# Three layers of one Trainium2 kernel: from three blocks to one block with handed-over beginnings

## The reference, cut to what matters

```python
x = x + L0(x)   # attention, 16 heads; dense or sparse per batch, by u_prev
x = x + L1(x)   # gates and causal running sums ("traces"), then a layer norm
x = x + L2(x)   # gelu(x W1 + b1) times W2, and a part of W2 chosen per batch ("expert")
x = x + L3(x)   # softmax((x + embed[stage]) keys^T) keys

# L1, cut:
ctx = causal_ema(x, tau_ctx)
gated = x * sigmoid([x, ctx] Wg^T + bg)
mod = 0.5 + sigmoid(gelu(x Wn1^T + bn1) Wn2^T + bn2)             # 32 columns
temporal = sum_d softmax(blend)_d * causal_ema(gated * mod_d, tau_d)   # 32 decays
out = (gelu(x Wsoma^T) * sigmoid(temporal Wtemp^T)) Wout^T
return layernorm(out) * gamma + beta
```

## Time and profile before

| | before |
|---|---|
| median of 3 runs | 1950.69 us (1947.42 to 1953.83) |
| the profiled execution | 1952.55 us, span 1950.9 us |
| attention layer (to its last value product) | 0 to 741.5 us |
| first layer edge (to `lags(0, 0, 0)`) | 741.5 to 785.2 us |
| trace layer's loop (to the last `turn_back`) | 785.2 to 1404.5 us |
| second layer edge (to `output(0, ., 0)`) | 1404.5 to 1453.3 us |
| last part | 1453.3 to 1950.9 us |
| busy: PE, DVE, ACT, POOL | 93%, 76%, 61%, 36% |

### The profile page before, as it was taken

One profiled execution on the slowest core, in us unless ns is written; L12 is line 12 of the kernel. 1 busy time (PEld: TensorE's weight loads), 2 busy tenths in 40 slices (PEclk: granted clock), 3 DMA queues, 4 the chain that ended last, 5 costly groups with the idle time before them and its releaser, 6 DMA issues. The chain is left out here.

```text
span 1950.9 us, 44118 instructions
## 1 busy us (share of the span) xinstructions
PE 1814.3 (93%) x14926; PEld 1462.5 (75%) x14926; DVE 1486.1 (76%) x2206; ACT 1194.9 (61%) x2493; POOL 711.0 (36%) x690
## 2 busy tenths in 40 slices
PE   4899999999999995999999999999749999999997
PEld 4566666666666653788888888888649999999997
DVE  6888998899889996878787878787526666666664
ACT  2677777777777764466666666666535555555553
POOL 5255555555555544333333333334101111111111
PEclk9999999999999996999999999999969999999998
DMA  3233333333333331000000000000031222222221
GB/s 101 92 121 125 110 119 119 124 114 115 122 121 116 114 95 46 1 1 0 0 0 0 0 0 0 0 0 0 1 97 58 80 88 74 73 73 78 86 78 47
DMA packets 104946, 126.25 MB, mean 65 GB/s; under 512 B 27840, under 2 KB 70464, under 8 KB 104896
## 3 DMA queue, kind: packets, MB, share of 16 engines
q1 hardware_dynamic: 86912, 102.72, 16.3%
q0 software_dynamic: 17408, 22.61, 3.7%
q10 hardware_dynamic: 576, 0.26, 0.1%
HBM read 56.54 MB, written 9.44 MB: 34 GB/s over the span
## 5 line engine op out<-in xcount | busy, mean ns | idle before, releaser
L445 DVE TENSOR_REDUCE a_top<-a_s 128x4 f32<-128x1024 f32 x256 | 309.7, 1211 | 75.6 <-PE a_s L708 68.6
L561 ACT ACTIVATE a_e<-a_t 128x512 f32<-128x512 f32 x512 | 276.1, 590 | 134.5 <-PE a_t L722 133.9
L455 DVE SCALAR_TENSOR_TENSOR a_e<-a_e,a_w_t 128x1024 f32<-128x1024 f32 x256 | 316.1, 1236 | 4.7 <-ACT a_e L561 4.7
L1818 ACT ACTIVATE c_hid<-c_pH,c_b 128x256 f32<-128x256 f32 x256 | 107.4, 471 | 189.5 <-PE c_pH L1881 189.1
L1058 POOL TENSOR_TENSOR b_decayed<-b_scratch,b_mod_t 128x1024 f32<-128x1024 f32 x64 | 124.1, 1962 | 206.5 <-ACT b_mod_t L1276 206.5
L737 PE MATMUL a_v<-a_e,a_v_pad 128*32 128x256 f32 x2048 | 165.4, 396 | 23.7 <-DVE a_e L455 20.9
L1442 PE MATMUL b_pS<-b_gated_t,b_decayed 128*128 128x256 f32 x768 | 183.3, 389 | 1.5 <-issue 0.2
L1881 PE MATMUL c_pH<-c_x_hi,c_w_hi 128*128 128x256 f32 x512 | 151.0, 295 | 22.3 <-DVE c_w_lo L1783 22.1
L703 PE MATMUL a_s<-a_absent,a_eye 64*128 64x512 bf16 x1024 | 156.8, 385 | 7.3 <-DMA a_absent<-b_bl_rep 5.4
L1696 POOL TENSOR_TENSOR c_w2b_lo<-c_we,c_w2b_hi 128x512 fp32r<-128x512 f32 x32 | 54.6, 1707 | 290.0 <-ACT c_w2b_hi L1811 290.0
L1442 PEld LDWEIGHTS b_pS<-b_gated_t,b_decayed 128*128 128x128 f32 x768 | 142.0, 192 | 24.1 <-issue 7.0
(11 more groups left out here) (273 smaller groups left out, 5447.1 us busy)
## 6 DMA issues: line engine op xcount, KB each, us to landing
a_st<-a_split SPq DMA_DIRECT2D x384, 128.0 KB, 2.1
b_wsoma<-in_xT SPq DMA_DIRECT2D x32, 256.0 KB, 3.7
x_all<-in_xT SPq DMA_DIRECT2D x32, 256.0 KB, 3.7
a_r_rep<-a_r_rows POOLq DMA_DIRECT2D x64, 128.0 KB, 3.7
c_we<-in_we SPq DMA_DIRECT2D x32, 256.0 KB, 2.8
c_key_t<-in_keyT SPq DMA_DIRECT2D x32, 256.0 KB, 3.2
c_value<-in_key SPq DMA_DIRECT2D x32, 256.0 KB, 2.7
out<-c_y POOLq DMA_DIRECT2D x32, 256.0 KB, 3.2
```

What stands on the lines that cost most here:

```text
L445: dve.tensor_reduce(top[:, qc, half].rearrange("p (r j c) -> p r j c", r=2, j=2)[:, :, cc], ps_s[g % 2][:], AX.X, ALU.max)\
L455: dve.scalar_tensor_tensor(out=buf[:], in0=buf[:], scalar=BIG, in1=w_t[par][:, kc].unsqueeze(1).to_broadcast([P, 4, S]), op0=ALU.min, op1= ...
L561: act.activation(e[g % E_BUFS][:, 2 * r:2 * r + 2], ps_t[r][:], ACT.Exp).then_inc(exp_done, 1)
L1818: ins = act.activation(hid[r % 2][:, i], pH[r][:, i], ACT.Gelu, bias=b1[:, 2 * r + i:2 * r + i + 1])
```

## The change

The three layers stand in one `Block`. Each layer's function now returns its engines' programs instead of running them; those of the second and third layer are generators. An engine's attention program gets the trace program as `then`, and calls `next(then)` at fixed places of its tail; each call emits the trace program's instructions up to its next `yield`. The trace program does the same with the last part's program. What remains is emitted at the end (`finish`). So a layer's tail and the next layer's head stand mixed in one instruction stream per engine.

The comments at the right of the added lines are put in here and say what the call emits; a call of `next(then)` in a last part's stretch works alike.

```diff
     # attention, GpSimd, after the batches
-        for half in range(2):
-            denominators(NB - 1, 1, half)
+        denominators(NB - 1, 1, 0)
+        next(then)                  # memset h1, low_x(0), low wn1, low wg
+        denominators(NB - 1, 1, 1)
         residual(NB - 3)
         compact(NB - 1)
         merge(NB - 1, 1)
+        next(then)                  # low_context(0)
         reciprocal_rows(NB - 1)
+        next(then)                  # decays(0, 0), low_x(1, 1)
         spread(NB - 1)
+        next(then)                  # low_context(1), low wsoma, low wtemp
         residual(NB - 2)
         residual(NB - 1)
-        pool.wait_ge(x1_done, NB)
...
     # attention, VectorE, after the batches
         weigh(NB - 1, 1, GROUPS - 1)
-        ahead_steps = trace_vector(dve, ahead)
-        next(ahead_steps)
+        next(then)                  # context(0), w_rep, w_lag
         normalize(NB - 2, 0)
-        next(ahead_steps)
         reciprocal(NB - 1)
-        next(ahead_steps)
+        next(then)                  # modulation(0), gating(0), low_steps, context(1), body(0) to lag_sum 2
         normalize(NB - 1, 1)
-        next(ahead_steps)
...
     # attention, TensorE, after the batches
+        next(then)                  # turn bl_rep
         mix_values(NB - 1, 1, GROUPS - 2)
         mix_values(NB - 1, 1, GROUPS - 1)
+        next(then)                  # hidden(0, 0)
         for n in (NB - 2, NB - 1):
             for m in range(C):
                 project_out(n, n % 2, m)
+            if n == NB - 2:
+                next(then)          # gate_in(0) ... turn(0), body(0) to modulate_rows(1)
...
     # trace, VectorE
+            if is_batch(n, NB - 1):
+                next(then)          # in body(31), after lag_sum 3: low w1, low_x(0)
...
-        loop(dve, body)
+        yield from loop(dve, body)
+        next(then)                  # split(0, 0)
         low_temporal(NB - 1)
+        next(then)                  # low parts of w2a and of the first w2b
         mixing(NB - 1)
+        next(then)                  # split(0, 1), low part of the second w2b
         low_mixed(NB - 1)
+        next(then)                  # split(0, 2), low_x(1), split(0, 3)
         norm(NB - 1)
...
     # trace, TensorE
+            if is_batch(n, NB - 1):
+                next(then)          # in body(31), after states 3: hidden(0, ., 0)
...
+        next(then)                  # hidden(0, ., 1), hidden(0, ., 2)
         gate_out(NB - 1)
+        next(then)                  # hidden(0, ., 3), hidden(1, ., 0), output(0, ., 0)
         output(NB - 1)
+        next(then)                  # hidden(1, ., 1), output(0, ., 1), hidden(1, ., 2), output(0, ., 2)
         turn_normed(NB - 1)
...
     # build_program
+        with nc.Block() as block:
+            @block.vector
+            def _(dve):
+                last = final.vector(dve)
+                second = trace.vector(dve, last)
+                attention.vector(dve, second)
+                finish(second)
+                finish(last)
```

More of the change, by code:

```diff
@@ L609, in body @@
                     projected(n - 2)
+                if g == 4 and not maxi:
+                    next(ahead_steps)
+                if g in (3, 6) and not maxi:
+                    next(then)
         act.wait_ge(set_up, LAM)
@@ L879, in trace_vector @@
     taus = [(tile["tau_c"], ahead.sp_c), (tile["tau_col"], ahead.sp_col), (tile["tau_row"], ahead.sp_row)]
-    blend_t, wout, table = tile["blend_t"], tile["wout"], ahead.table
+    blend_t, table = tile["blend_t"], ahead.table
     def link(ins):
@@ L892, in trace_vector @@
         link(dve.tensor_scalar(tau[:], tau[:], 80.0, None, ALU.min))
-    link(dve.tensor_reduce(ahead.bl_max[:], blend_t[:], AX.X, ALU.max, negate=True))
     yield
@@ L898, in trace_vector @@
     yield
+    dve.wait_ge(ahead.d_tab, 16 * len(TRACE_TABLES) + 16)
+    link(dve.tensor_reduce(ahead.bl_max[:], blend_t[:], AX.X, ALU.max, negate=True))
     dve.wait_ge(ahead.a_set, 2)
@@ L1087, in _, with vector @@
         low_weight(1, wg, wg_p)
+        yield
         low_context(0)
+        yield
+        decays(0, 0)
+        before.mixed_all(pool)
+        low_x(1, 1)
+        yield
+        low_context(1)
         low_weight(2, wsoma, wsoma_p)
         low_weight(3, wtemp, wtemp_p)
-        decays(0, 0)
-        low_context(1)
-        loop(pool, body)
+        yield
+        yield from loop(pool, body)
+        next(then)
         residual(NB - 1)
-        pool.wait_ge(x2_done, NB)
-    @block.vector
-    def _(dve):
+    def vector(dve, then):
         done = [0]
@@ L1543, in _ @@
         turn(0, 0)
-        pe.wait_ge(w_lo, 4)
-        pe.wait_ge(set_done, 1)
-        loop(pe, body)
+        before.banks_free(pe, "columns")
+        pe.wait_ge(early_done, 2)
+        yield from loop(pe, body)
+        next(then)
         gate_out(NB - 1)
+        next(then)
         output(NB - 1)
+        next(then)
         turn_normed(NB - 1)
+    return handover, Programs(None, gpsimd, vector, scalar, tensor)
 HIDDEN = 1024
@@ L1680, in body, with gpsimd @@
             if ahead:
-                load(n + 1, 1 - par)
-        load(0, 0)
-        loop(sp, body)
-    @block.gpsimd
-    def _(pool):
+                if not is_batch(n, 0):
+                    load_expert(n + 1, 1 - par)
+                load_keys(n + 1, 1 - par)
+            yield from ()
+        before.gates_all(sp)
+        sp.dma_start(w2[:], t["w2"].rearrange("(k p) e -> p k e", p=P)).then_inc(d_w2, 16)
+        load_expert(0, 0)
+        load_expert(1, 1)
+        before.states_all(sp)
+        sp.dma_start(embed_all[:], t["embed"].partition_broadcast(P)).then_inc(d_emb_all, 16)
+        before.added(sp, NB)
+        sp.wait_ge(d_emb_all, 16)
+        load_keys(0, 0)
+        yield from loop(sp, body)
+    def gpsimd(pool):
         def store(n, par):
@@ L1943, in body @@
                 mix_values(n - 1, 1 - par)
-        for r in range(ROUNDS):
-            hidden(0, 0, r)
-        pe.wait_ge(w_lo, 2)
-        loop(pe, body)
+        before.banks_free(pe, "pA")
+        pe.wait_ge(w_lo, 1)
+        hidden(0, 0, 0)
+        yield
+        before.banks_free(pe, "pL0")
+        hidden(0, 0, 1)
+        before.banks_free(pe, "pL1")
+        hidden(0, 0, 2)
+        yield
+        before.banks_free(pe, "pS")
+        hidden(0, 0, 3)
+        yield from loop(pe, body)
         scores(NB - 1, 1)
```

567 lines of the change are left out of this document (381 added, 186 removed).

## The result

| | before | changed |
|---|---|---|
| median | 1950.49 us (4 runs, 1947.42 to 1953.83) | 1918.89 us (4 runs, 1918.04 to 1919.72) |
| ratio | | 0.9829, 95% interval 0.9817 to 0.9840 |
| profiled span | 1950.9 us | 1916.6 us |
| busy PE, DVE, ACT, POOL | 93%, 76%, 61%, 36% | 95%, 77%, 62%, 37% |

The forecast was 1905.5 us, with 1891 to 1923 as its range. The kernel is 31.6 us faster by the medians and 34.3 us by the profiled spans, where 45.8 us were forecast. The busy row of the page hardly moves, as it should: the same work is done, and the time comes out of idling.

A forecast was written before the change was run, and what follows sets the result against it. TensorE, busy 93% of the span, bounds the kernel, with 60 us of its idling at the edges. 18 + 29 - 1.2 = 45.8 us off the profiled 1952.55 gives 1906.8, forecast as 1905.5 us, range 1891 to 1923.

The forecast's parts named there:

- Loops: The three layers' loops: instructions and order stay the same, rounds unchanged to 0.05 us.
- Start: Kernel start: small transfers queued beside the weights and ScalarE's small exponentials lose 1.2 us.
- First edge: Attention layer to trace layer: mixing their tail and head wins 18 us, bounds 10 to 26 us.
- rival A: First edge: the round trip holds up TensorE, each layer waiting for the other; 8 of 18 us left, 1916 us; chance 0.14.
- the half microsecond for `centred_output` and the low part of wout: First edge, VectorE in batches 0 and 1: some 2 us of work mostly fits, costing 0.5 us.
- Second edge: Trace layer to last part: wins 29 us from block end, w1 load and filled last chain; bounds 22 to 35 us.
- Rival B: Second edge: its gap is traded for another by strict engine order; 18 of 29 us kept, 1917 us; chance 0.12.
- The barrier: Block's end at the second edge: 9.5 us of idling, counted inside the 29 us gain.
- rival D: The barrier was hidden anyway, or engines meet at new waits as at the old: no change, 1950 us; chance 0.02.
- rival E: Loops slow as tiles move in memory: 0.5 us a batch cancels the gain, 0.6 us gives 1961 us; chance 0.03.
- Rival C: Both edges: filled, they keep TensorE off the low clock, worth 9 us; 1896 us; chance 0.14.
- The forecast's 2 us of contention: First edge: 2 us added for VectorE's `w_lag` beside GpSimd's work; by the Skill's rule about 4 us instead.

The follow-up runs named there:

- before_placed: The kernel before, with the last part's tiles allocated at the changed kernel's places in main memory; 1955.16 us in one run, last part's round 15.378 us.
- early_dve: Changed kernel with the centring of wout and w_st's low part on VectorE between normalize(30) and reciprocal(31); 1921.01 us.
- seq2: Changed kernel with the second handover undone: the last part's program is emitted whole behind the trace layer's on every engine; 1930.10 us.
- both_edges: Changed kernel with edge2_full and edge1_full together, and normalize(31) moved behind the second states of batch 0; 1903.33 us.
- edge2_full: x12_early with batch 0's residual and queries ahead of split(1, 1), and the keys' loads waiting for the trace layer's last output products; 1906.58 us.
- edge1_full: Changed kernel with centring in attention batch 31, w_st's low part behind reciprocal(31), w1's load waiting for the trace layer's first residual; 1918.02 us.
- x12_early: Changed kernel with the high and low parts of x(1) and x(2) made earlier in ScalarE's and VectorE's order at the second edge; 1909.86 us.
- psum_swap: Changed kernel with the banks of two partial-sum tiles, pO and pH3, exchanged; 1919.06 us, last part's round 15.385 us.

## Why the forecast was right in kind and 13 us off in size

Against the profiled execution the forecast expected 45.8 us, and the spans gave 34.3, so 11.5 us are missing. The rest of the 13.4 us between the forecast of 1905.5 us and the median is scatter between profiled executions and medians (the one before lay 1.9 us above its median of that time, that of the changed kernel 0.3 us below), 0.3 us by which the changed kernel's execution is longer beyond its span, and a slip: 1906.8 less 1.9 is 1904.9, not 1905.5. The prediction had also named two signs of its being wrong. The first, edges that give under 27 us together, did not come: they gave 38.8. The second, a loop's round that has moved, did: see "Loops". The terms, each by its own name:

- **Start**, forecast 1.2 us lost: 0.4 us at the last copy. It can't be told apart from the 3.9 us by which the attention layer's end moved between runs.
- **First edge**, forecast 18 us, measured 14.1. The marks came about where they had been named: `lags` forecast at 762 to 766 and seen at 764.53, `spread(0, 0)` at 775 and seen at 775.82, TensorE's wait for att under 5 us and seen at 0.85 (rival A, the round trip, did not come). That they fit so well is in part luck, since links of the chain were off in both directions (GpSimd, then VectorE):

```profile
744.45 2.49 POOL L1152 TENSOR_TENSOR b_wn_lo<-b_wn,b_wn_hi 128x128 fp32r<-128x128 f32 x1
758.27 4.01 POOL L1160 TENSOR_TENSOR b_decayed<-b_scratch,b_mod_t 128x1024 f32<-128x1024 f32 x2 [2.75 <-ACT b_mod_t L1418]
```
```profile
743.33 3.30 DVE L1225 TENSOR_TENSOR w_early<-b_w_rep,b_power 128x2048 f32<-128x2048 f32 x1
758.95 2.20 DVE L1253 SCALAR_TENSOR_TENSOR b_gated<-b_th_g,x_all 128x512 f32<-128x512 f32 x1 [1.52 <-ACT b_th_g L1399]
761.18 3.25 DVE L1232 TENSOR_TENSOR b_w_st<-w_early,b_w_st 32x2048 fp32r<-32x2048 f32 x1
```

  The low part of wn took 2.49 us beside `w_lag`, where it took 0.50 before, and the three low parts ended at 749.7 and not at 748. `decays` took 4.01 us and not 5.56, and ended at 762.3 and not at 765. Then `low_x(1)` waited 1.40 us for ScalarE, and VectorE, in batch 0's own products, took up att at 773.16 where the sum has 771.2. Counted from the last copy, `spread(0, 0)` gained 16.9 us, where the sum's times say 18.3 (792.31 less 774; its 18.5 is a slip of 0.2). These are 1.4 us of the shortfall. The other 2.3 us are the step that failed most clearly, the half microsecond for `centred_output` and the low part of wout inside batches 0 and 1. I had counted their 2 us as fitting into VectorE's idling, but they stood directly ahead of temporal(0), for which `gate_out(0)` waits:

```profile
785.87 0.67 DVE L1237 TENSOR_REDUCE b_mean_w<-b_scratch 128x2 f32<-128x512 f32 x1
786.58 0.17 DVE L1238 TENSOR_SCALAR b_mean_w<-b_mean_w 128x2 f32<-128x2 f32 x1
786.78 0.74 DVE L1240 TENSOR_SCALAR b_scratch<-b_scratch,b_mean_w 128x256 f32<-128x256 f32 x2
787.56 0.69 DVE L1293 TENSOR_TENSOR b_temporal<-b_inner,b_pY 128x512 f32<-128x512 f32 x1
...
789.56 0.68 DVE L1297 TENSOR_TENSOR b_temp_lo<-b_temporal,b_temp_hi 128x512 fp32r<-128x512 f32 x1
```
```profile
790.30 0.39 PE L1564 MATMUL b_pY<-b_temp_hi,b_wtemp_hi 128*128 128x256 f32 x1 [2.02 <-DVE b_temp_lo L1297]
```

  The wait is 2.0 us, and behind it the clock fell (the granted clock was 0.50 from 792.2 to 794.2). early_dve puts the price of the placing at 2.5 us.
- **Second edge**, forecast 29 us, measured 24.7. The loop's end came 2.4 us late (forecast 2.8). The first gap was forecast at 5.4 us from 1412.9 and is 5.98 us from 1412.7 (old count, 13.3 us added). The second gap, implied at 2.9 us between 1433.2 and 1436.1, is 4.4 us: ScalarE's gelus wait for GpSimd's residual, which they do not read, and the sum had left this out:

```profile
1420.34 1.57 ACT L2047 ACTIVATE c_hid<-c_pH,c_b 128x256 f32<-128x256 f32 x4 [1.40 <-POOL x_all L1166]
```

  And I let TensorE come back at full speed; its next twelve products and eight scores take 5.5 us in the chain above, against 3.2 in the kernel before (1465.13 to 1468.32). At `hidden(2, ., 0)` itself, for which the 29 us were forecast, the edge had given 26.7; that product came 40.0 us earlier than in the kernel before, not 45. Rival B, a gap traded for another, was a matter of degree.
- **The barrier.** seq2 shows 13.6 us for it and the loads behind it; its 9.5 us of idling and the 10.3 us to the first product had been put in that sum together with the mixing, and rival D falls.
- **Loops**, forecast no change "to 0.05 us": the trace layer's round moved by 0.02 us, which is what it moves between runs that leave this loop alone (19.417 to 19.433 us in the changed kernel and its variants), the last part's by 0.107. This is rival E's mechanism, other places in memory, at a fifth of the size from which it would have decided; before_placed shows it in the kernel before. I had no row for it and gave it no term: 3.2 us of the error.
- **The clock.** Rival C needed the edges full. At 0.84 and 0.87 they were not; both_edges filled the second, and the granted clock there went to 1.00; C had priced the clock alone at 9 us; edge2_full, which filled that edge too, shortened it by 12.5 us with the gaps themselves in that number.

Of the shared access of VectorE and GpSimd, the Trainium skill (SBUF — State Buffer, section "Who interferes with whom") says that a VectorE instruction with two inputs in that memory is blocked by a GpSimd instruction that reads it. By that rule the trace agrees: 2.78 us instead of 0.68 with two such inputs, 0.69 with one. The forecast's 2 us of contention did not cover the chain before `lags`: the low part of wn (2.49 us for 0.50), `gating` (2.20 for 0.66) and the low part of `w_st` (3.25 for 2.28) lost 4.5 us together, near the 4 us that the prediction had worked out by the rule. What the runs add is that the loser can wait through a series of GpSimd instructions, and need not: the same addition of batch 0 took 4.58 us in early_dve, 3.46 in edge1_full and 1.25 in the changed kernel, beside the same four products, and ended each time 0.48 us after one of them. Instructions of another form were held too: the scaling of `mean_w` (2.03 us for 0.17) and the rounding `c_hid_hi` (1.50 for 0.42).

## What to carry to other kernels

Two layers may stand in one stream, but each moved piece has to be placed by what waits behind it on its engine: a rounding of data 550 us old cost 6 us because of where it stood. Price a moved piece by the longest row that the trace has for it beside the neighbouring engine's work, and look for the next link before you call a gap closed: x12_early closed 4.4 us and kept 1.1. When tiles are moved in memory, compare the durations of the loop's own instructions, since 2% on a weight load is invisible in a timeline and adds up over 32 batches.

## What the runs showed of the hardware that was not expected

- Weight loads of 128x128 in fp32r took a median of 188 or 192 ns by where the layer's tiles stand in the main memory alone, all else the same (before_placed); the bank of the partial sums made no difference (psum_swap).
- A GpSimd series held one VectorE instruction for 2.1 us (both_edges), 2.8 us (edge1_full, 3.46 against 0.62 us) and 4.0 us (early_dve, 4.58 against 0.62 us). That GpSimd was what held it is inferred from the ends, 0.48 to 0.56 us after the series' own.
- A load of 1 MB on SyncE's queue beside the last round trip had the transfer engines busy to 771 us, and without it they were free at 769; yet att started at 773.16 and 773.41 all the same, since VectorE was in steps of the trace layer's batch 0 until then in both, so this collision, which I had suspected, cost nothing there.
